# A fused attention and expert kernel: keys and queries of two head groups projected as two 64-row products side by side

## The reference

```python
c_q = x @ W_DQ
Qc = (c_q @ W_UQ)   # 16 heads of 8
Qr = rope(c_q @ W_QR)   # 16 heads of 4
c_kv = x @ W_DKV
Kc = (c_kv @ W_UK)
Kr = rope(x @ W_KR)   # shared by the heads
V = (c_kv @ W_UV)
scores = jnp.clip(einsum('bhqd,bhkd->bhqk', [Qc, Qr], [Kc, Kr]), -80.0, 80.0)
weights = softmax(where(causal, scores, -inf) / sqrt(12))
x = layernorm(x + (weights @ V) @ W_O)
e = argmax(x @ gate_w.T + gate_b + expert_bias)
x = layernorm(x + relu(x @ w1[e] + b1[e]) @ w2[e] + b2[e])
```

## Time and profile before

| | |
|---|---|
| time, median of 3 runs | 467.28 us (465.78 to 469.02) |
| profiled execution, its own time | 468.31 us |
| its span, first to last instruction | 466.6 us |
| mean granted TensorE clock | 0.978 |

### The profile page before, as it was taken

How to read it: one execution, slowest core, us unless ns; L and a number is a source line. 1 busy time by engine, 2 the same in 40 slices (tenths; PEclk the granted TensorE clock), 3 DMA queues, 4 the chain that set the end, 5 groups by cost and what they waited for, 6 DMA issues and landing times. The chain is left out here.

```text
span 466.6 us, 12398 instructions
## 1 busy us (share of the span) xinstructions
PE 430.2 (92%) x4259; PEld 233.6 (50%) x4259; DVE 370.6 (79%) x838; ACT 348.1 (75%) x548; POOL 166.9 (36%) x165
## 2 busy tenths in 40 slices
PE   7899999999999999999999999997999899699980
PEld 5543443434344344344443443443444798599970
DVE  4598789989896988989799889999888388366670
ACT  0697887988779888887988988787987554466650
POOL 8112112106315211431512115322002566688882
PEclk9999999999999999999999999998999899899995
DMA  3746647845442570156118305443410356577710
GB/s 100 193 124 147 156 122 152 205 128 126 102 94 68 131 162 6 42 119 138 46 35 187 77 1 136 91 99 89 115 25 1 93 145 165 156 185 212 196 55 6
DMA packets 33181, 51.67 MB, mean 111 GB/s; under 512 B 5675, under 2 KB 16337, under 8 KB 33120
## 3 DMA queue, kind: packets, MB, share of 16 engines
q1 hardware_dynamic: 25504, 37.04, 34.0%
q10 hardware_dynamic: 5344, 9.57, 7.3%
q0 software_dynamic: 2272, 4.27, 2.7%
HBM read 20.82 MB, written 5.33 MB: 56 GB/s over the span
## 5 line engine op out<-in xcount | busy, mean ns | idle before, releaser
L950 ACT ACTIVATE prob<-ring 128x1024 f32<-128x1024 f32 x288 | 273.9, 1036 | 44.9 <-PE ring L1096 43.7
L1114 PE MATMUL o_acc<-prob,v_stat 128*32 128x512 f32 (+3 forms) x1536 | 154.5, 497 | 3.2 <-DVE prob L626 2.5
L1096 PE MATMUL ring<-queries,keys 32*128 32x512 f32 (+3 forms) x1536 | 122.5, 382 | 0.9 <-ACT prob L950 0.9
L1096 PEld LDWEIGHTS ring<-queries,keys 32*128 32x128 f32 x1536 | 66.5, 184 | 72.8 <-issue 43.2
L519 POOL CAST parts<-whole_kq 128x512 fp32r<-128x512 f32 x32 | 39.1, 1221 | 139.0 <-DVE whole_kq L594 139.0
L626 DVE SCALAR_TENSOR_TENSOR prob<-prob,mask_hi 128x1024 f32<-128x1024 f32 (+1 forms) x80 | 86.1, 1076 | 0.0
L612 DVE TENSOR_SCALAR prob<-prob 128x2048 f32<-128x2048 f32 x64 | 77.4, 1220 | 7.2 <-ACT prob L950 6.2
L1023 ACT ACTIVATE prob<-ring,b1T 128x128 f32<-128x128 f32 x156 | 44.5, 368 | 38.0 <-PE ring L1214 16.8
L625 DVE TENSOR_SCALAR prob<-prob 128x1024 f32<-128x1024 f32 (+1 forms) x80 | 63.4, 793 | 11.8 <-ACT prob L950 11.6
L527 POOL DMA_INDIRECT by_expert<-xrow,index x32 | 42.9, 1341 | 50.9 <-DVE index L721 43.1
L1114 PEld LDWEIGHTS o_acc<-prob,v_stat 128*32 128x32 f32 x1536 | 34.1, 109 | 51.2 <-issue 34.0
(11 more groups left out here) (106 smaller groups left out, 312.7 us busy)
## 6 DMA issues: line engine op xcount, KB each, us to landing
queries<-parts SPq DMA_DIRECT2D x62, 256.0 KB, 3.9
v_stat<-in_w ACTq DMA_DIRECT2D x34, 256.0 KB
keys<-parts SPq DMA_DIRECT2D x64, 128.0 KB, 2.4
queries<-by_expert SPq DMA_DIRECT2D x39, 66.0 KB
xrow<-in_x_rows SPq DMA_DIRECT2D x8, 264.0 KB, 4.2
xT<-in_x_T SPq DMA_DIRECT2D x8, 256.0 KB
v_stat<-in_w SPq DMA_DIRECT2D x5, 256.0 KB
out<-prob,queries POOLq DMA_INDIRECT x39
```

Of the source, the lines that this page charges most:

```text
L950: act.activation(prob[u % P_SLOTS][:, 2 * half:2 * half + 2, :].rearrange("p h s -> p (h s)"), slot(u, half)[:], ACT.Exp, scale=SCALE).the ...
L1096: last = pe.matmul(out[:, j % 2 * QC + off:j % 2 * QC + off + w], keys[hg][r, kt * P:(kt + 1) * P], queries[hg][r, qc, part, QC - w:QC], s ...
L1114: last = pe.matmul(o_acc[j * VW:(j + 1) * VW, QC - w:QC], v_stat[b % 2][:, hg, kt, j, :], prob[u % P_SLOTS][:, j, off:off + w], start=begi ...
```

## The change

Keys and queries of both head groups of a pair are now made by one `project` job (pair, half of the sequence), four for each sequence, 16 in all. It is two products, each 64 rows deep: rows 0 to 63 of `w_kq` and `latent` give the keys of both groups (128 output rows), rows 64 to 127 the queries of both. They go to the two banks of one slot of the scores' ring, so a project takes its turn as a fill of the ring (`FILLS`), between the unit's scores and its `weigh`; it waits until the slot is free (`claim_ring`), and whoever fills the slot next waits for it in turn.

The keys need no rotary factor and go straight from PSUM: ScalarE copies them to the upper part (`upper_of_keys`), VectorE subtracts from PSUM for the lower part (`lower_of_keys`). The queries are still multiplied into SBUF by VectorE (`turn_queries`), and GpSimd makes their upper part (`upper_of`), VectorE their lower part (`lower_of_queries`). The ring slot is free when `turn_queries` and `lower_of_keys` are done. In VectorE's order that is: `turn_queries(u)`, `clip(u)`, `lower_of_keys(u)`, then in the next turn `clip(u + 1)`, `lower_of_queries(u)`.

The jobs move: projects now stand at n = 1 and 6 (own pair 1) and at n = 19 and 24 (pair 0 of the next sequence). Before the first unit there are two instead of three, and in the first sequence's units two (at 4 and 8) instead of five, and its second `v` is at unit 1 instead of 3. The first project's copy of the queries is ScalarE's too. Each project is followed by eight DMAs of SyncE in a row instead of four; their number in all is the same. VectorE no longer fills the keys' half of the rotary table with ones, and that table is loaded by four DMAs instead of two. TensorE's filler products between the first jobs are 12 instead of 8 each, into `o_acc`. A few small tiles of the experts' stage now lie in `prob[0]`, and VectorE waits for unit 140's `weigh` ahead of that stage.

```diff
-OWN_JOBS = {0: ("project", 2, 0), 2: ("project", 3, 0), 6: ("project", 2, 1), 8: ("project", 3, 1),
+OWN_JOBS = {1: ("project", 1, 0), 6: ("project", 1, 1),
...
              [job_at(b, n) for b in range(B) for n in range(UB) if job_at(b, n)] + TAIL_JOBS)
-MISC_NO = {job: i for i, job in enumerate(MISC_JOBS)}
 PROJECTS = [job[1:] for job in MISC_JOBS if job[0] == "project"]
 PROJECT_NO = {project: i for i, project in enumerate(PROJECTS)}
+MISC_JOBS = [job for job in MISC_JOBS if job[0] != "project"]
+MISC_NO = {job: i for i, job in enumerate(MISC_JOBS)}
+def fills():
+    out = [numbered(job, 0) for job in FIRST_JOBS if job[0] == "project"]
+    for u in range(B * UB):
+        out += [("score", u, 0), ("score", u, 1)] + ([step_job(u, "project")] if step_job(u, "project") else [])
+    return out
+FILLS = fills()
+FILL_NO = {fill: i for i, fill in enumerate(FILLS)}
...
-        whole_kq = [sb(f"whole_kq{i}", [P, QC]) for i in range(2)]
-        parts = [sb(f"parts{i}", [P, 2, QC], F32R) for i in range(2)]
+        whole_q = [sb(f"whole_q{i}", [P, QC]) for i in range(2)]
+        key_parts = [sb(f"key_parts{i}", [P, 2, QC], F32R) for i in range(2)]
+        query_parts = [sb(f"query_parts{i}", [P, 2, QC], F32R) for i in range(2)]
...
-        def slot(u, half):
-            return ring[(2 * u + half) % RING_SLOTS]
+        def slot(fill):
+            return ring[FILL_NO[fill] % RING_SLOTS]
...
+        def rows_of_group(hg):
+            return slice(hg % 2 * QROW, (hg % 2 + 1) * QROW)
         def spread_keys(eng, b, hg, c):
+            i = PROJECT_NO[b, hg // 2, c]
             for part in range(2):
                 eng.dma_start(keys[hg][part:P:2, c * QC:(c + 1) * QC].bitcast(F32),
-                              parts[PROJECT_NO[b, hg, c] % 2][0:QROW, part, :].bitcast(F32)).then_inc(kq_in[hg][c], 16)
+                              key_parts[i % 2][rows_of_group(hg), part, :].bitcast(F32)).then_inc(kq_in[hg][c], 16)
         def spread_queries(eng, b, hg, c):
+            i = PROJECT_NO[b, hg // 2, c]
             for row in range(2):
                 eng.dma_start(queries[hg][row:P:2, c].bitcast(F32),
-                              parts[PROJECT_NO[b, hg, c] % 2][QROW:P].bitcast(F32)).then_inc(kq_in[hg][c], 16)
+                              query_parts[i % 2][rows_of_group(hg)].bitcast(F32)).then_inc(kq_in[hg][c], 16)
...
+        def parts_spread(eng, i):
+            if i >= 2:
+                b, pair, c = PROJECTS[i - 2]
+                for hg in (2 * pair, 2 * pair + 1):
+                    eng.wait_ge(kq_in[hg][c], (b + 1) * 64)
...
-            def spread(b, hg, c):
-                sp.wait_ge(lower_part, PROJECT_NO[b, hg, c] + 1)
+            def spread(b, pair, c):
+                sp.wait_ge(lower_keys, PROJECT_NO[b, pair, c] + 1)
                 if b:
-                    sp.wait_ge(scored, 2 * ((b - 1) * UB + (hg // 2 + 1) * NU))
-                spread_keys(sp, b, hg, c)
-                spread_queries(sp, b, hg, c)
+                    sp.wait_ge(scored, 2 * ((b - 1) * UB + (pair + 1) * NU))
+                for hg in (2 * pair, 2 * pair + 1):
+                    spread_keys(sp, b, hg, c)
+                sp.wait_ge(lower_queries, PROJECT_NO[b, pair, c] + 1)
+                for hg in (2 * pair, 2 * pair + 1):
+                    spread_queries(sp, b, hg, c)
...
-            def upper_of(b, hg, c):
-                i = PROJECT_NO[b, hg, c]
-                pool.wait_ge(proj_out, i + 1)
-                if i >= 2:
-                    b0, hg0, c0 = PROJECTS[i - 2]
-                    pool.wait_ge(kq_in[hg0][c0], (b0 + 1) * 64)
-                pool.tensor_copy(parts[i % 2][:, 0, :], whole_kq[i % 2][:]).then_inc(upper_part, 1)
+            def upper_of(b, pair, c):
+                i = PROJECT_NO[b, pair, c]
+                pool.wait_ge(queries_out, i + 1)
+                parts_spread(pool, i)
+                pool.tensor_copy(query_parts[i % 2][:, 0, :], whole_q[i % 2][:]).then_inc(upper_queries, 1)
...
-            def turn_queries(b, hg, c):
-                i = PROJECT_NO[b, hg, c]
+            def turn_queries(b, pair, c):
+                i = PROJECT_NO[b, pair, c]
                 dve.wait_ge(projected, i + 1)
                 if i >= 2:
-                    dve.wait_ge(lower_part, i - 1)
-                dve.tensor_tensor(whole_kq[i % 2][:], misc[:], rope_q[:, c * QC:(c + 1) * QC], ALU.mult
-                                  ).then_inc(proj_out, 1)
-            def lower(b, hg, c):
-                i = PROJECT_NO[b, hg, c]
-                dve.wait_ge(upper_part, i + 1)
-                dve.tensor_tensor(parts[i % 2][:, 1, :], whole_kq[i % 2][:], parts[i % 2][:, 0, :], ALU.subtract
-                                  ).then_inc(lower_part, 1)
+                    dve.wait_ge(lower_queries, i - 1)
+                dve.tensor_tensor(whole_q[i % 2][:], slot(("project", b, pair, c))[:, QC:2 * QC],
+                                  rope_q[:, c * QC:(c + 1) * QC], ALU.mult).then_inc(queries_out, 1)
+            def lower_of_keys(b, pair, c):
+                i = PROJECT_NO[b, pair, c]
+                dve.wait_ge(upper_keys, i + 1)
+                dve.tensor_tensor(key_parts[i % 2][:, 1, :], slot(("project", b, pair, c))[:, 0:QC],
+                                  key_parts[i % 2][:, 0, :], ALU.subtract).then_inc(lower_keys, 1)
+            def lower_of_queries(b, pair, c):
+                i = PROJECT_NO[b, pair, c]
+                dve.wait_ge(upper_queries, i + 1)
+                dve.tensor_tensor(query_parts[i % 2][:, 1, :], whole_q[i % 2][:], query_parts[i % 2][:, 0, :],
+                                  ALU.subtract).then_inc(lower_queries, 1)
...
                     before_clip(*job_at(u // UB, u % UB))
                 clip(u)
+                if step_job(u, "project"):
+                    lower_of_keys(*step_job(u, "project")[1:])
                 if step_job(u - 1, "project"):
-                    lower(*step_job(u - 1, "project")[1:])
+                    lower_of_queries(*step_job(u - 1, "project")[1:])
...
+            def upper_of_keys(b, pair, c):
+                i = PROJECT_NO[b, pair, c]
+                act.wait_ge(projected, i + 1)
+                parts_spread(act, i)
+                act.activation(key_parts[i % 2][:, 0, :], slot(("project", b, pair, c))[:, 0:QC], ACT.Copy
+                               ).then_inc(upper_keys, 1)
...
             for u in range(B * UB):
...
                 exp(u, 1)
                 if u >= LAG and last_unit(sums_of(u - LAG)) == u - LAG:
                     o_evac(sums_of(u - LAG))
-                if job_at(u // UB, u % UB):
+                if step_job(u, "project"):
+                    upper_of_keys(*step_job(u, "project")[1:])
+                elif job_at(u // UB, u % UB):
...
-            def project(b, hg, c):
-                claim_misc(("project", b, hg, c))
+            def claim_ring(fill):
+                n = FILL_NO[fill] - RING_SLOTS
+                if n >= 0 and FILLS[n][0] == "score":
+                    _, u, half = FILLS[n]
+                    pe.wait_ge(exped, 2 * u + half + 1)
+                elif n >= 0:
+                    pe.wait_ge(queries_out, PROJECT_NO[FILLS[n][1:]] + 1)
+                    pe.wait_ge(lower_keys, PROJECT_NO[FILLS[n][1:]] + 1)
+            def project(b, pair, c):
+                fill = ("project", b, pair, c)
+                claim_ring(fill)
                 pe.wait_ge(latent_out, NQC * b + c + 1)
-                pe.matmul(misc[:], w_kq[:, hg, :], latent[:, c * QC:(c + 1) * QC], start=True, stop=True
-                          ).then_inc(projected, 1)
+                for i in range(2):
+                    r = slice(i * Q0, (i + 1) * Q0)
+                    last = pe.matmul(slot(fill)[:, i * QC:(i + 1) * QC], w_kq[r, pair, :],
+                                     latent[r, c * QC:(c + 1) * QC], start=True, stop=True)
+                last.then_inc(projected, 1)
...
-                    out = slot(u, half)
-                    if 2 * u + half >= RING_SLOTS:
-                        pe.wait_ge(exped, 2 * u + half - RING_SLOTS + 1)
+                    out = slot(("score", u, half))
+                    claim_ring(("score", u, half))
...
-                warm(8)
+                warm(12)
             for u in range(B * UB):
                 score(u)
+                if step_job(u, "project"):
+                    project(*step_job(u, "project")[1:])
                 if u >= LAG:
                     weigh(u - LAG)
-                if job_at(u // UB, u % UB):
+                if job_at(u // UB, u % UB) and not step_job(u, "project"):
```

91 lines of the change are left out of this document (46 added, 45 removed).

## The result

The changed kernel takes 469.93 us (median of 19 runs, 467.44 to 470.93) against 467.28 for the kernel before; the ratio is 1.005, with a 95% interval of 1.0036 to 1.0064. Its profiled execution has a span of 468.4 us, for 466.6. The forecast was 459.7. TensorE's mean granted clock is 0.960, for 0.978.

A forecast was written before the change was run, and what follows sets the result against it. TensorE was taken as the bound in units with jobs, ScalarE by little in those without, VectorE in some stretches. Gains 1.9 + 3 x 0.2 + 3 x 0.9 + 3 x 0.8 = 7.6 us gave a 459.7 median, range 457 to 464.

The forecast's parts named there:

- The pair of products side by side, 1.06: TensorE's two 64-row products of a project overlap and take 1.06 us for both, as one product before.
- the rival: The two products run one after the other, 1.06 us more per pair, 10.5 in all, 470.2 us; chance 0.12.
- ScalarE's copy 0.6, hidden: ScalarE's copy of the keys from PSUM takes 0.63 us, hidden where ScalarE would idle about 0.8 in a project's unit.
- Place A: Units 108 to 113, n = 1: TensorE waits 1.3 us for `lower_of_keys`; two projects become one, gaining 0.2 in each of three sequences.
- Place B: Units 114 to 117, n = 6 and 8: no ring wait, unit 116 loses its project, gaining 0.9 us in each of three sequences.
- Places C and D: Units 90 to 93 (n = 18 to 20) and 95 to 98 (n = 23 to 25): 0.8 us gained together, in three sequences.
- The first sequence: Start and first units: unit 0 begins at about 15.9 us instead of 17.11; net gain 1.9 by unit 14.
- an unseen thing of 0.05: Something not foreseen, of either sign, such as TensorE's half-clock stretches falling elsewhere; chance 0.05.
- The sum: Whole kernel: gains add to 7.6 us, 468.3 to 460.7 for a profiled execution, 459.7 for the median.
- the ring wait takes it all: Rival: each `lower_of_keys` comes 0.8 us later than walked, at nine places, 7.2 in all; 467 (465 to 469), chance 0.18.

The follow-up runs named there:

- e10_serial: The changed kernel with both products of a pair on rows 0 to 63, so they cannot run side by side: 475.87 us, ratio 1.0206 to the kernel before.
- e7_hold: Fillers at the start and behind the scores of units 0 to 2, added to the changed kernel with products at steps 6, 8, 25, 31: 461.33 us, 462.93 without.
- e12_best: The changed kernel with `lower_of_keys` ahead of the clip, the next sequence's second pair at step 25, and fillers in the first units: 454.85 us, ratio 0.9747.
- e5_order: The changed kernel with `lower_of_keys` ahead of the unit's clip on VectorE instead of behind it: 459.67 us, ratio 0.9846 to the kernel before.
- e14_masked: The changed kernel with `lower_of_keys` ahead of the clip in masked units alone: 459.70 us, ratio 0.9882 to the kernel before.
- e2_fill: The changed kernel with 24 filler products ahead of the scores of unit 3 of sequences 1 to 3: 467.06 us, ratio 1.0003 to the kernel before.
- e13_order25: The changed kernel with `lower_of_keys` ahead of the clip and the next sequence's second pair at step 25, no fillers: 457.27 us, ratio 0.9837.

## Why the prediction was wrong, step by step

- **The pair of products side by side, 1.06.** Right: 1.13, and e10_serial prices the rival at 5.9 us (7 by the ratios), where it was put at 10.5. Most of its error is at A, where the wait hides it, as the rival itself said.
- **ScalarE's copy 0.6, hidden.** Right: behind it ScalarE still idles for scores, 0.56 us at A and D, 0.57 at C, 0.24 at B. But ScalarE's other copy, of `o_acc`, was not in the account.
- **Place A, "it waits 1.3 ... the place gives 0.2".** This is the step that failed most. The mechanism was right and walked instruction by instruction; two sizes were not. The wait is 1.82: TensorE is there when the walk says (6.58 us behind unit 108's scores, for 6.59), but `lower_of_keys` is 0.5 late, 0.4 of which is the mask instruction, 1.63 beside GpSimd's copy and not the 1.22 of a clip that stands alone. The trace of before had that length at the same place. And the time behind the wait was reckoned at full clock: in two of three sequences TensorE's idling was followed by half clock, 1.1 to 1.4 us more each. It lost 1.67, 1.67 and 0.61 for a gain of 0.2 each, 4.6 us of the forecast's 7.6. In the last sequence, where the clock held, the miss is 0.8.
- **Place B, 0.9.** Right: 1.1.
- **Places C and D, 0.8.** C's wait was put at 0.7 and is 1.22 (0.4 of it again the mask instruction, 1.64), and D's gain, put at 0.7, is 0.2 in sequences 1 and 2, because step 24 leaves the copy of `o_acc` uncovered (0.77). Together the two places lost 0.2 in those sequences and gained 0.2 in the first, for a gain of 0.8 each. The walk asked which slot TensorE would get and never who covered the copy that the removed project had stood in front of. With step 25 and the order mended D gives 0.84 and C 0.06, 0.9 together: the forecast's size.
- **The first sequence, 1.9.** Unit 0 began at 16.70, not 15.9, since only then had the DMA of its queries landed. Even the 0.4 us that it came earlier is not shown to be a gain: in the nine traces that have the changed kernel's start unit 0 begins at 16.70 to 17.73, 17.2 on average, for 17.11 before. Behind it the forecast expected 0.7 and got -1.57. By e7_hold 2.3 us are the half clock that follows TensorE's idle time at the start; with clock and order mended those units give 1.29 (e12_best), of which its later unit 0 takes 0.7 back. The prediction named slow stretches only as an unseen thing of 0.05. The trace of before had its clock full there, and I took that as given; yet removing TensorE's work is what lets it idle (1.28 us busy of 14.40 to 17.80, rows above).
- **The sum.** The forecast's profiled execution was 7.6 us faster than the one before, the measured one is 1.8 slower. Of that miss about 4.6 are at A, 3.1 in the first sequence and 2.6 at C and D; B gave 0.6 more than forecast. The forecast's 459.7 is what e5_order measures, but that is chance: its units 0 to 14 lose 1.2 where the forecast has a gain of 0.7, its places A gain 0.8 each for 0.2, and 1.2 us are a slow stretch that its trace lacks.
- **The rival "the ring wait takes it all"**, 467 at 0.18, came nearest, and the wait that it named is the one that was seen. But it put 0.8 us at nine places. The wait is 0.5 longer than walked at A and at C, and at D there is none: 3.1 us of its 7.2. The rest of the miss is the clock and the copy of `o_acc`, which it did not have, and the measured 469.9 lies above its 465 to 469 as well.
- The prediction weighed a rule of the Trainium skill, TensorEngine Tiling (Array Packing), Performance Considerations: packing speeds up TensorE, not the emptying of PSUM, which may become the bottleneck (the page says it of a fourfold speedup). The trace agrees: it was the emptying on which the ring hung (10.1 us in 7 waits), by its place in VectorE's queue and not by its own 0.68 us.

The cause is shown for A and C (e5_order, e14_masked), for the clock (e2_fill, e7_hold) and for D (e13_order25, by its trace). It is not shown why the same 1.8 us of idle time is followed by half clock in sequences 1 and 2 and not in the last. Open too is the experts' stage, the same code in all versions of the changed kernel: from unit 143 to the end it takes 110.2 us in the trace before, 110.0 after, 108.2 in e5_order, 107.9 in e12_best and 106.6 in e14_masked, so that differences of 1 to 3 us between two runs can lie there.

## What to carry to other kernels

When a job's output moves into a resource that the next work needs, put the instruction that gives it back ahead of whatever else stands in its engine's queue: here one subtraction put ahead of the clip is worth 10 us by the medians, 8 at the places that it touches, and turns 0.5% slower into 1.5% faster. Price a wait of TensorE not by its length alone but also by the clock in the work behind it, above all where the change takes away TensorE's own work. And when a job is moved away, ask what it stood in front of.
